# Where VectorE loads eight chunk places into registers: behind its last operation of a step, or behind the second addition

## The reference, cut to what matters

```python
q_att = jnp.einsum('nhd,rhde->rnhe', q, relation_att)
v_msg = jnp.einsum('nhd,rhde->rnhe', v, relation_msg)
aw_q_edge = q_att[etype, col_idx]
msg_edge = v_msg[etype, row_idx]
attn_score = jnp.sum(aw_q_edge * k[row_idx], axis=-1)
score = attn_score * (relation_pri[etype] / SQRT_DK)
m = jax.ops.segment_max(score, col_idx, num_segments=n)
ex = jnp.exp(score - m[col_idx])
denom = jax.ops.segment_sum(ex, col_idx, num_segments=n)
alpha = ex / denom[col_idx]
agg = jax.ops.segment_sum(alpha[..., None] * msg_edge, col_idx, num_segments=n)
```

## Time and profile before

| | |
|---|---|
| median of 3 runs | 2159.93 us |
| profiled execution, its own time | 2155.21 us |
| span of that execution | 2153.9 us |
| granted TensorE clock, mean | 0.963 |
| busy: PE, DVE, ACT, POOL | 88%, 76%, 68%, 55% |
| DVE's loads of eight places | 55, the first at 613.9 us, the last at 1770.3 us |

### The profile page before, as it was taken

One profiled execution on the slowest core, in us unless ns is written; L12 is line 12 of the kernel. 1 busy time (PEld: TensorE's weight loads), 2 busy tenths in 40 slices (PEclk: granted clock), 3 DMA queues, 4 the chain that ended last, 5 costly groups with the idle time before them and its releaser, 6 DMA issues.

```text
span 2153.9 us, 37341 instructions
## 1 busy us (share of the span) xinstructions
PE 1885.7 (88%) x10336; PEld 1428.7 (66%) x10336; DVE 1637.1 (76%) x3979; ACT 1460.9 (68%) x4926; POOL 1189.2 (55%) x1207
## 2 busy tenths in 40 slices
PE   6999998998689999998999999999999873926999
PEld 6865555555567777777778777777777752614666
DVE  8757776654589999989989999998999985873111
ACT  7855555554378888888889887888888863831221
POOL 0033334432776777777777776777777703502554
PEclk9999999999899999999999999999999996956999
DMA  7958888999999999989999999999999917671221
GB/s 237 324 188 324 316 321 278 370 363 369 299 319 300 315 313 304 311 295 300 307 296 320 317 311 300 303 306 302 314 306 319 311 45 231 193 269 50 75 76 43
DMA packets 271461, 583.71 MB, mean 271 GB/s; under 512 B 45078, under 2 KB 185962, under 8 KB 264600
## 3 DMA queue, kind: packets, MB, share of 16 engines
q0 software_dynamic: 93936, 384.51, 51.4%
q1 hardware_dynamic: 177320, 196.82, 28.2%
HBM read 407.81 MB, written 176.99 MB: 272 GB/s over the span
## 4 chain that ended last, share of the span: by engine, by line
PE 54%; DVE 23%; issue 11%; DVEq 3%; POOL 3%; ACT 3%; DMA 3%; SPq 0%; POOLq 0%; ACTq 0%
PE bank L985 9%; PE bank L804 7%; PE bank L969 6%; PE bank L1143 4%; PE bank L1154 4%; PE bank L783 4%; PE bank L865 4%; DVE arena L1972 3%; DVE arena L2065 3%; PE bank L950 3%; POOL arena L2378 3%; DVE arena L2029 3%; PE bank L650 2%; PE bank L706 2%; PE bank L694 2%
## 5 line engine op out<-in xcount | busy, mean ns | idle before, releaser
L2378 POOL DMA_INDIRECT arena<-table,arena x880 | 874.8, 994 | 327.5 <-issue 253.5
L1355 ACT ACTIVATE arena<-arena 128x64 f32<-128x64 f32 x3432 | 839.7, 340 | 0.0
L985 PE MATMUL bank<-arena 128*128 128x260 f32 x1760 | 436.0, 391 | 45.2 <-DVE arena L2065 42.1
L985 PEld LDWEIGHTS bank<-arena 128*128 128x128 f32 x1760 | 321.0, 191 | 122.2 <-issue 74.3
L1972 DVE TENSOR_TENSOR arena<-bank,arena 128x512 f32<-128x512 f32 x440 | 300.4, 685 | 71.9 <-PE bank L969 45.1
L969 PE MATMUL bank<-arena 128*128 128x256 bf16 x2640 | 335.2, 275 | 7.5 <-DVE arena L1972 7.5
L969 PEld LDWEIGHTS bank<-arena 128*128 128x128 bf16 x2640 | 258.3, 99 | 64.0 <-DVE arena L1972 8.9
L1982 DVE TENSOR_REDUCE arena<-arena 128x16 f32<-128x1024 f32 x220 | 268.0, 1218 | 20.7 <-DVE arena L1972 0.9
L804 PE MATMUL bank<-arena 64*128 64x512 f32 x832 | 207.2, 613 | 17.0 <-DVE arena L1717 11.9
L1237 ACT COPY arena<-bank 128x512 f32<-128x512 f32 x260 | 149.1, 595 | 81.7 <-PE bank L804 81.0
L2065 DVE TENSOR_TENSOR arena<-arena,bank 128x260 f32 x440 | 184.3, 419 | 7.6 <-PE bank L985 2.4
(11 more groups left out here) (324 smaller groups left out, 2975.5 us busy)
## 6 DMA issues: line engine op xcount, KB each, us to landing
arena<-q_parts SPq DMA_DIRECT2D x440, 192.0 KB
arena<-chunk_rel SPq DMA_DIRECT2D x220, 128.0 KB, 5.4
arena<-table,arena POOLq DMA_INDIRECT x880, 5.1
node_rows<-arena SPq DMA_DIRECT2D x24, 512.0 KB, 6.3
xl_and_sum<-arena SPq DMA_DIRECT2D x3, 3072.0 KB, 18.2
arena<-in_x SPq DMA_DIRECT2D x12, 512.0 KB, 7.7
xn<-arena SPq DMA_DIRECT2D x12, 512.0 KB, 8.0
xT<-arena SPq DMA_DIRECT2D x12, 512.0 KB, 8.1
```

Of the source, the lines that this page charges most:

```text
L985: ins = TE.matmul(bank[b][:, 0:AW], lhsT=so[p % 2][:, c % 2, j, :], rhs=values_of(c, j), start=j == 0, stop=j == HALF - 1)
L1355: ins = A.activation(seg, seg, ACT.Copy, scale=rows[:, C + h:C + h + 1])
L2378: G.indirect_dma_start(rows_of_pair(p, i % 2 * HALF + j), None, d_tab_rows[0:N * R, :], bass.IndirectOffsetOnAxis(ap=idxE[:, g, j, c:c + 1 ...
```

## The change

`load_places` moves within its step. Before, it stood behind `edge_targets` (and, in the last 14 steps, behind `weigh`), ahead of the pieces of mix. Now it stands directly behind the second addition, ahead of the second product. The number of loads, their contents and the steps that have them are the same, and no other engine's instructions change place.

```diff
             for i in range(2):
                 if a >= 0:
                     add_chunk(2 * a + i)
+                if i == 1 and 2 * (a + 1) % PLACES == 0 and 0 <= a + 1 < NPAIR:
+                    load_places(2 * (a + 1) // PLACES)
                 if p < NPAIR:
                     product(p, i)
...
             if SHARED + WEIGH_LAG <= p < NPAIR + WEIGH_LAG:
                 weigh(p - WEIGH_LAG)
-            if 2 * (a + 1) % PLACES == 0 and 0 <= a + 1 < NPAIR:
-                load_places(2 * (a + 1) // PLACES)
             next(work, None)
```

## The result

The changed kernel took 2200.21 us (median of 5 runs, 2199.13 to 2204.83), the kernel before 2159.93 us (5 runs beside it, 2155.94 to 2164.44). The ratio is 1.0192, with a 95% interval of 1.0173 to 1.0211: slower by 41 us, 37 to 46. The forecast was 2200 us, its sum +42 us.

What follows compares the result with a forecast made beforehand. PE (93% busy) and DVE (92%) were taken to swap the bound from step to step; 41 - 2 + 2.5 = 42 us on the time before gave 2200 us, range 2188 to 2212 (8 times in 10: 2175 to 2221).

Steps and rivals of the forecast that it cites:

- That the load is covered today, and by what: At the old place, 1.22 + 0.35 + 0.69 us of work handed over before (reduction, one-hot, targets), less overlaps, hides the load.
- Lateness of 1.26 us for each load: Second product in the load's step starts at 1120.94 instead of 1119.68 us; everything behind it on DVE is late too.
- 36 loads pay, 15 don't: Full steps: lateness reaches PE where addition end and waiting scatter's start are under 0.14 + 1.26 us apart; 36 of 51 loads.
- 0.88 to 1.29 us for each of the 36: Loss behind each paying load in the full steps, 1.15 us in the mean, 41 us together.
- Minus 2 us for PE's waits for ACT: PE waits 13.7 us for ACT's exponential in 13 places; late scatters can use up such waits, so 2 us off.
- The last 14 steps, 2.5 us: Steps without products: targets and weighing would start behind the load; three loads at 0.8 us, 2.5 us.
- The very first load: Load at the start of the additions, no addition ahead of it: between 0 and 1.3 us, taken as 0.
- PE's waits for L2065 grow from 34.6 to about 70 us: Sign of the forecast: PE's scatter waits longer for DVE's addition, from 34.6 to about 70 us.
- Mostly absorbed: Rival: DVE's idle time in the stage uses up most lateness; 5 to 28 us, 2160 to 2186 us; chance 0.13.
- DVE becomes the bound: Rival: in the stage nearly every load is paid, +58 to +72 us, 2215 to 2230 us; chance 0.08.
- The load is short at the new place: Rival: with less work queued ahead the load takes 0.6 us, under the second addition; cost 0, 2158 us; chance 0.04.
- Faster: Rival: 4.7 us of issue idling goes, load falls into second product's wait for PE; 2150 to 2155 us; chance 0.03.

Runs made afterwards that it cites:

- twice_again: Kernel of twice_new timed again (load written twice in a row at the new place; profile shows 55 loads, not 110), against the kernel before: 2201.94 us, ratio 1.0193.
- twice_new: Changed kernel with the load written twice in a row at the new place; ratio 1.0055 to the kernel before, which took 2421.94 us in that series.

## Why the prediction was right, point by point

*That the load is covered today, and by what.* Right. The load at the old place costs nothing to be seen, and a shorter one there gives nothing back (0.9990).

*Lateness of 1.26 us for each load.* Right: 1.25 us in the step compared, 64.6 us of idle time in front of 52 products, forecast "some 50 times, about 60 us".

*36 loads pay, 15 don't.* Right, and this was the step that could have failed most easily. It was tested by moving either set alone: 1.0167 and 0.9999. The 36 gave 36 us (32 to 40) where the sum had 41 - 2 = 39. The reason given for the 15 is not the whole one. Behind five of them the distance from addition to scatter is 1.15 or 1.16 us in the trace before, under the 1.40 us of the rule. Behind load 9, one of these, DVE itself idles before that addition, longer than it can be late:

```profile
819.90 0.69 DVE L1972 TENSOR_TENSOR arena<-bank,arena 128x512 f32<-128x512 f32 x1 [1.92 <-PE bank L969]
```

So room is either a distance or idle time of the late engine on the way.

*0.88 to 1.29 us for each of the 36.* Right in the mean only: 40.2 us over 36 are 1.12 each, forecast 1.15. Single loads go from 0.0 to 2.7 us, and seven of the 36 show 1.5 us or more, which is more than their lateness of 1.25 us can be.

*A term that the sum doesn't have: the granted clock.* In the trace before, PE's clock is at its lower level (1.2 of 2.4 GHz) in four stretches of 3.4 us between the start of step 13 and the last product, in the trace after in nine. One of the nine lies behind load 44. The four steps from this load to the next took 20.84 us before, 23.59 us after and 21.93 us in the second profiled execution of the same changed kernel (the run `twice_again`), which has no such stretch there, nor has the one before. After, then in that second execution:

```profile
1610.13:1633.72 23.59, 21.50 (x118) 17.46 (x117) 20.42 (x44) 17.80 (x71) 15.72 (x16) 0.93 0.87 291
```

```profile
1607.51:1629.44 21.93, 19.85 (x118) 16.61 (x117) 20.23 (x44) 17.81 (x71) 14.97 (x16) 1.00 0.92 310
```

With the same 118 matmuls PE is busy 21.50 us against 19.85. The load cost 1.1 us there and the clock 1.7. By this, the five further stretches are worth at most 5 x 1.7 = 8.5 us (an estimate) of the 40.1. PE's own figures agree in kind: of the 40.1 us it was idle for 27.2 and busier by 12.9. So in the profiled pair lateness behind the 51 loads gave some 30 to 37 us (38.8 less 8.5, or less the 1.7 seen; an estimate), under the 39 of the sum, and the clock made up for it: the total came out so near in part by luck. How much of this is in the medians stays open: the mean clock of a whole execution was 0.953 to 0.958 after, and 0.952 to 0.963 in all those before near 2160 us. What brings on the lower clock is not shown either.

*Minus 2 us for PE's waits for ACT.* The sign was right, the size small: those waits fell from 13.7 us in 13 places to 7.3 in 9, by 6.4 us. In the trace of the 36 alone they are 9.0 us in 9 places, 4.7 us less.

*The last 14 steps, 2.5 us.* Under-sized in the profiled pair: 5.5 us. Part of it is the clock, 0.89 there against 0.96: three stretches of 3.4 us at the lower level against one, at most 3.4 us by the same estimate, and PE is busy 3.4 us longer there (34.77 against 31.42). What is left, 2.1 us, is near the forecast. *The very first load*, put at 0, took 1.3 us, the upper end that the prediction gave it.

*The mark "PE's waits for L2065 grow from 34.6 to about 70 us".* Too simple. In the stretch 620 to 1780 us they are 58.2 us. The rest of the lateness is met by PE elsewhere: its transposes L650 wait 34.9 us for DVE's L1927, a piece of mix, where the row for such waits before was lower (23.3 us in 620 to 1780). I had followed lateness to the additions only. That the sum holds all the same could be because a step that is late at L650 would have been late at the scatter otherwise, so that PE pays once; no run separates the two.

*The rivals.* "Mostly absorbed" is what happened to the 15 loads, and to much of it in the series at 2421.94 us, where the changed kernel (as `twice_new`) lost 13 us. Its bounds were also added up wrongly: 5 to 28 us on 2160 give 2165 to 2188, not 2160 to 2186. "DVE becomes the bound" didn't: 29.5 us of waits for PE's expansion are left. "The load is short at the new place" is refuted by 1823 ns at the least. The Trainium skill, "DMA: Bandwidth & Descriptors", section "Latency and other measured facts", has about 600 ns as a floor; two places took 502 ns at the least, so here the floor is lower. The Trainium skill, "Runtime: NRT & Kernel Launch", section "Instruction fetch mechanics", has about 200 ns a register, on a page that speaks of loads from HBM; these loads read SBUF, and eight took 1830 ns, 229 ns each. "Faster" had no support: the issue idling it would have removed was replaced by more.

## What to carry to other kernels

In this kernel a register load was free where the work handed to the engine before it lasted longer than it did: 1.83 us behind the targets, 0.51 us behind the second addition. Put such a load behind the longest such run of work, or make it shorter than the work in front. Of lateness that remains, count only the places where another engine stands right behind the late one, and where the late one has no idle time of its own on the way: 15 idlings of 1.2 us cost nothing, 36 cost 1.0 us each (36 us). Look at PE's busy time and granted clock on both sides too, before the whole difference is put down to waiting. And where something else holds the stage up, such a change can look like little (1.0055 instead of 1.0193); look at the time of the kernel before first.

## What the runs showed of the hardware that was not expected

- A TENSOR_LOAD of two 16-bit places on DVE took 506 ns, one of four 948, one of eight 1830: 441 or 442 ns for each further pair, and 65 ns besides. A single place on POOL took 507 ns, as long as two on DVE, which speaks for a price by pairs and not by places; whether POOL's and DVE's loads can be compared wasn't measured.
- Not every load takes the same time: of the 55 on DVE before, five took 2.2 to 2.9 us. Why wasn't found.
- On one chip (number 9) the kernel before took 2422 us instead of 2160, and in the trace of the 15 from that series the products wait 170.6 us for something untraced. Why wasn't found.
- A stretch of 3.4 us at the lower clock cost the edge stage 1.7 us, where it could be compared (load 44).
- A wait put down to an engine whose work had ended 0.68 us before (the reduction behind the product) was in truth the sequencer's load; the view of one line doesn't say so, the instruction order does.
